# First attention of a gated two-layer network: preparation spread anew over its visits, value bias moved to the turned output

## The reference, cut to what matters

```python
kv = concat([y_main @ Wk + bk, y_main @ Wv + bv])      # per head 16 keys, 16 values
k = _ln(kv[..., :HD], kn_w, kn_b);  v = kv[..., HD:]
q = _ln((x @ Wq + bq).reshape(b, s1, H, HD), qn_w, qn_b)
ctx = _attn(q, k, v) + _attn(q, k_dca, v_dca)          # softmax(q k' * SCALE) v, each
x = x + tanh(g_xattn[0]) * (ctx @ Wo + bo)
```

## Time and profile before

| what | value |
|---|---|
| median of 3 runs | 1889.63 us (1887.51 to 1890.85) |
| profiled execution | 1893.01 us, its span 1891.3 us |
| mean granted TensorE clock | 0.981 of full speed |
| TensorE busy over the span | 1802.5 us (95%) |
| VectorE, ScalarE busy | 1420.0 us (75%), 1208.8 us (64%) |
| GpSimd busy | 352.2 us (19%) |

### The profile page before, as it was taken

How to read it: one execution, slowest core, us unless ns; L and a number is a source line. 1 busy time by engine, 2 the same in 40 slices (tenths; PEclk the granted TensorE clock), 3 DMA queues, 4 the chain that set the end, 5 groups by cost and what they waited for, 6 DMA issues and landing times.

```text
span 1891.3 us, 31855 instructions
## 1 busy us (share of the span) xinstructions
PE 1802.5 (95%) x9292; PEld 1334.9 (71%) x9292; DVE 1420.0 (75%) x2350; ACT 1208.8 (64%) x2035; POOL 352.2 (19%) x309
## 2 busy tenths in 40 slices
PE   5798898999999999999999999999999999999998
PEld 3444444568888767787777767778777777888887
DVE  8566656556666889897898988889889997666665
ACT  2576667853233778886888867888788885222222
POOL 3010101204444400001000010000100102454442
PEclk9799999989999999999999999999999999999999
DMA  3404141444443200001000010000000000544542
GB/s 98 109 19 109 32 96 35 93 159 126 111 116 89 70 1 1 0 0 35 1 1 0 0 35 1 1 0 0 1 22 1 0 17 16 114 109 106 116 114 75
DMA packets 108711, 95.90 MB, mean 51 GB/s; under 512 B 71796, under 2 KB 93176, under 8 KB 107992
## 3 DMA queue, kind: packets, MB, share of 16 engines
q1 hardware_dynamic: 108632, 94.88, 19.9%
HBM read 72.94 MB, written 1.44 MB: 39 GB/s over the span
## 4 chain that ended last, share of the span: by engine, by line
PE 83%; DVE 8%; ACT 2%; issue 2%; SPq 2%; POOL 1%; DMA 0%; DVEq 0%; ACTq 0%
PE ps L1308 36%; PE ps L472 17%; PE ps L484 8%; PE ps L1153 5%; PE ps L1140 4%; PE ps L1324 3%; PE ps L1078 2%; SPq L575 2%; PE ps L1389 1%; PE ps L1332 1%; PE ps L1417 1%; DVE s_rk L2015 1%; POOL s_p L811 1%; ACT s_p L1022 1%; DVE s_dsum L2091 1%
## 5 line engine op out<-in xcount | busy, mean ns | idle before, releaser
L1022 ACT ACTIVATE s_p<-ps,s_g,s_rk 128x256 f32<-128x256 f32 (+1 forms) x832 | 413.2, 561 | 8.9 <-DVE s_dsum L2091 7.6
L1308 PE MATMUL ps<-s_qq,s_ctxT 128*128 (+3 forms) x1248 | 357.9, 400 | 6.6 <-ACT s_p L1022 5.9
L472 PE MATMUL ps<-s_xT,s_wgus 128*128 128x512 f32 x1440 | 350.3, 392 | 0.0
L1308 PE MATMUL ps<-s_ps,s_ctx 128*128 128x512 f32 x1152 | 325.2, 395 | 0.9 <-DVE s_ps L2082 0.9
L472 PEld LDWEIGHTS ps<-s_xT,s_wgus 128*128 128x128 f32 x1440 | 271.2, 189 | 59.9 <-issue 1.5
L2082 DVE TENSOR_TENSOR s_ps<-s_p,s_ps 128x512 fp32r<-128x512 f32 x384 | 269.1, 701 | 20.8 <-ACT s_ps L1030 17.4
L899 ACT ACTIVATE s_p<-ps,s_bsm 128x1024 f32<-128x1024 f32 x208 | 219.5, 1111 | 88.7 <-PE ps L1153 86.3
L1308 PEld LDWEIGHTS ps<-s_qq,s_ctxT 128*128 128x128 f32 (+1 forms) x1248 | 224.0, 185 | 67.7 <-ACT s_p L1022 9.5
L1308 PEld LDWEIGHTS ps<-s_ps,s_ctx 128*128 128x128 f32 x1152 | 216.1, 188 | 56.6 <-DVE s_ps L2082 4.2
L2091 DVE TENSOR_TENSOR s_dsum<-s_dsum,s_p 128x512 f32<-128x512 f32 (+1 forms) x352 | 241.9, 687 | 16.5 <-ACT s_p L1022 12.8
L1886 DVE TENSOR_TENSOR s_hs<-s_hw,s_hs 128x512 fp32r<-128x512 f32 x120 | 140.6, 1172 | 80.6 <-ACT s_hs L383 80.6
(11 more groups left out here) (269 smaller groups left out, 2053.7 us busy)
## 6 DMA issues: line engine op xcount, KB each, us to landing
s_wB<-w1s SPq DMA_DIRECT2D x64, 256.0 KB, 3.9
s_kT<-s_kst SPq DMA_DIRECT2D x96, 128.0 KB, 2.4
s_kT<-s_kst SPq DMA_DIRECT2D x96, 80.0 KB, 2.1
s_wB<-w0s SPq DMA_DIRECT2D x15, 384.0 KB, 3.5
s_wB<-w0s SPq DMA_DIRECT2D x16, 256.0 KB, 3.8
s_wgu<-in_L_ffn_Wg_dram SPq DMA_DIRECT2D x64, 64.0 KB, 2.8
s_wgu<-in_L_ffn_Wu_dram SPq DMA_DIRECT2D x64, 64.0 KB, 2.5
s_wd<-in_L_ffn_Wd_dram SPq DMA_DIRECT2D x64, 64.0 KB, 2.4
```

Source lines behind the costliest of these rows:

```text
L472: ins = nc.tensor.matmul(ps[:, 4 + g, :], WGUS[f][:, slot, w, g, k, :], XT[f][:, x_, k, n], start=c == 0, stop=c == len(ops) - 1)
L1022: ins = nc.scalar.activation(p1[0:r, SLOT1[t], j, :], ps[0:r, BANK1[t], j * SQ:(j + 1) * SQ], ACT.Exp, bias=g1[0:r, 3:4], scale=rk_col(t, ...
L1308: ins = nc.tensor.matmul(out, lhs(x_), rhs(y_), start=first and n == 0, stop=last and n == 2)
```

## The change

1. `visit_work`: the 13 projections go two to a visit from visit 4 to 11 (where the second place isn't taken by `sums` or `query`); the keys of the next batch's half 0 go to visits 16 to 19, its query to visit 21. VectorE's list is reordered to match. `SQUARE` and `ROOT` move to earlier steps.
2. In a visit TensorE issues the values of the visit's first step before the second piece, not after it.
3. The bias of the values is not added to them. It is loaded as a column (`vb0`, 32 small loads), the two parts are summed, and it is added where the turned output is taken from PSUM.
4. In the prologue ScalarE copies the values of batch 0 and all four turned chunks of x; VectorE reads a tile only after ScalarE has (`v0_read`). ScalarE also writes the rounded part of the first keys; VectorE reads the first queries before the last two key tiles.
5. `center` multiplies and subtracts in one operation.

```diff
-TURN_ACT = (0, 2, 5, 7, 9)
-TURN_DVE = (0, 2, 3, 5, 7)
+TURN_ACT = (0, 4, 7, 9, 11)
+TURN_DVE = (0, 0, 1, 3, 5)
...
     if more:
-        first.update({4 + t: ("proj", b + 1, t) for t in range(KT)})
-        first.update({20: ("keys", b + 1, 0, 0), 21: ("query", b + 1, 0), 22: ("keys", b + 1, 0, 3)})
-        second.update({20: ("keys", b + 1, 0, 1), 21: ("keys", b + 1, 0, 2)})
+        places = [(work, u) for u in range(4, 12) for work in (first, second) if u not in work]
+        for t, (work, u) in enumerate(places[:KT]):
+            work[u] = ("proj", b + 1, t)
+        first.update({16 + c: ("keys", b + 1, 0, c) for c in range(4)})
+        first[21] = ("query", b + 1, 0)
...
-SQUARE = (18, 27, 35, 37)
-ROOT = 40
+SQUARE = (15, 21, 25, 28)
+ROOT = 32
...
+        def value_pieces(b, t):
+
+            pv = ps[:, misc_bank(MISC["proj", b, t]), :].rearrange("p (h two d) -> p h two d", two=2, d=D0)
+            return [(vg[r0:r0 + r, b % 2, tile, 0:H0 * (D0 + 1)].rearrange("p (h d) -> p h d", d=D0 + 1)[:, :, 0:D0], pv[r0:r0 + r, :, 1, :])
+                    for r0, r, tile in ([(0, P, t)] if t < KT - 1 else [(0, KREST, t), (DROW, DCA, KT)])]
...
+                if b == 0:
+                    for row in range(2):
+                        for c in range(KD):
+                            part = a["bkv0"][0, row, :].rearrange("(h two d) -> h two d", two=2, d=D0)[8 * c:8 * c + 8, 1, :]
+                            for h in range(8):
+                                sp.dma_start(vb0[D0 * h:D0 * h + D0, row, c:c + 1], part[h, :].rearrange("(p o) -> p o", o=1)).then_inc(s.vb_loaded, 16)
...
-            act_turn(act, 0)
+            def first_values(tiles):
+
+                for t in tiles:
+                    act.wait_ge(s.misc_made, MISC["proj", 0, t] + 1)
+                    for to, src in value_pieces(0, t):
+                        ins = nc.scalar.copy(to, src)
...
+                    ins.then_inc(s.v0_read, 1)
+
+            act_std(act, 0)
+            act.wait_ge(s.vg_ones, 1)
+            first_values(range(0, 4))
+            for half in range(2):
+                act_take(act, 0, half, (0, 1))
...
             for c in range(4):
+                if c < 3:
+                    first_values(range(4 * c + 4, min(4 * c + 8, KT)))
                 square(0, c)
...
-                    ins = nc.scalar.activation(p0[:, c, cols], ps[:, misc_bank(m), cols], ACT.Identity,
-                                               bias=wcol[:, 3 + 2 * j:4 + 2 * j], scale=wcol[:, 2 + 2 * j:3 + 2 * j])
+                    for to in (p0[:, c, cols], kst[:, 0, c * HALF + cols.start:c * HALF + cols.stop]):
+                        ins = nc.scalar.activation(to, ps[:, misc_bank(m), cols], ACT.Identity,
+                                                   bias=wcol[:, 3 + 2 * j:4 + 2 * j], scale=wcol[:, 2 + 2 * j:3 + 2 * j])
...
-                    prepare(second)
                     if tiles == 3:
                         scores_at(n + 5)
-                    for k in range(tiles):
+                    values(b, step)
+                    prepare(second)
+                    for k in range(1, tiles):
                         values(b, step + k)
...
+                if b == 0:
+                    dve.wait_ge(s.v0_read, t + 1)
...
-                me.did(v.tensor_tensor(kx[:, t], pv[:, :, 0, :], bv[:, :, 0, :], ALU.add))
-                if t < KT - 1:
-                    value(0, P, t).then_inc(s.misc_read, 1)
...
+                ins = v.tensor_tensor(kx[:, t], pv[:, :, 0, :], bv[:, :, 0, :], ALU.add)
+                if b:
+                    me.did(ins)
+                    pieces = value_pieces(b, t)
+                    for to, src in pieces:
+                        ins = v.tensor_copy(to, src)
...
-                cols = slice(starts[js[0]], starts[js[-1] + 1])
-                me.do(v.tensor_scalar(s1[:, cols], s1[:, cols], 1.0 / D0, None, ALU.mult))
                 for j in js:
-                    ins = v.tensor_tensor(centered[j][0], centered[j][0], bc(s1[:, starts[j]:starts[j + 1]], D0), ALU.subtract)
+                    ins = v.scalar_tensor_tensor(out=centered[j][0], in0=bc(s1[:, starts[j]:starts[j + 1]], D0), scalar=-1.0 / D0,
+                                                 in1=centered[j][0], op0=ALU.mult, op1=ALU.add)
...
-                v.tensor_copy(xnT[:, c, 0:HALF], ps[:, MISCBANK, :]).then_inc(s.misc_read, 1)
+                v.tensor_scalar(xnT[:, c, 0:HALF], ps[:, MISCBANK, :], vb0[:, 0, c:c + 1], None, ALU.add).then_inc(s.misc_read, 1)
```

More of the change, by code:

```diff
@@ L907, in _ @@
                 act.wait_ge(s.cx_turned, 4 * (c + 1))
-                nc.scalar.copy(xnT[:, c, HALF:2 * HALF], ps[:, 4 + c, :]).then_inc(s.cxT_act, 1)
+                if c == 0:
+                    act.wait_ge(s.misc_read, primed(MISC["ctx", 0] + 1))
+                nc.scalar.activation(xnT[:, c, HALF:2 * HALF], ps[:, 4 + c, :], ACT.Identity, bias=vb0[:, 0, c:c + 1]).then_inc(s.cxT_act, 1)
             def shares_exp(half):
@@ L1065, in bank_free @@
             def bank_free(m):
-                pe.wait_ge(s.misc_read, primed(m - 3 if m <= MISC["query", 0, 0] else m))
+                if m == MISC["query", 0, 0]:
+                    pe.wait_ge(s.kf_made, 1)
+                elif m < MISC["query", 0, 0]:
+                    pe.wait_ge(s.misc_read, primed(m - 3))
+                else:
+                    pe.wait_ge(s.misc_read, primed(m))
             def project(b, t):
@@ L1699, in read_keys @@
                 if b + half:
-                    dve.wait_ge(s.qz_ready, NG * b + (1 + (c == 3) if half else (c >= 2)))
+                    dve.wait_ge(s.qz_ready, NG * b + (1 + (c == 3) if half else 0))
                     dve.wait_ge(s.misc_made, m + 1)
@@ L1790, in _ @@
             scale_keys(0, 1)
-            for c in range(4):
-                read_keys(0, 0, c)
+            bounds()
+            read_keys(0, 0, 0)
+            read_keys(0, 0, 1)
+            dve.wait_ge(s.kf_made, 4)
+            dve.sem_inc(s.misc_read, 4)
             read_queries(0, 0)
-            bounds()
+            read_keys(0, 0, 2)
+            read_keys(0, 0, 3)
             for b in range(B):
@@ L1803, in _, with project @@
                 read_keys(b, 1, 3)
[L1804 to L1826 removed]
+                def project(tiles):
+                    if more:
+                        for t in tiles:
+                            read_projected(b + 1, t)
+                project(range(0, 4))
+                keep_sums(b, 0)
+                project(range(4, 7))
+                read_sums(b, 0)
+                if more:
+                    sum_squares(b + 1, 0)
+                project((7,))
+                read_queries(b, 2)
+                project((8, 9))
+                if more:
+                    sum_squares(b + 1, 1)
+                else:
+                    add_bias()
+                project(range(10, KT))
+                keep_sums(b, 1)
                 if more:
                     sum_squares(b + 1, 2)
+                read_sums(b, 1)
+                if more:
                     sum_squares(b + 1, 3)
                     key_variance(b + 1)
[L1831 removed]
+                read_queries(b, 3)
                 if more:
@@ L1835, in _ @@
                     scale_keys(b + 1, 1)
+                    read_keys(b + 1, 0, 0)
+                    read_keys(b + 1, 0, 1)
+                else:
+                    take_ctx(0)
+                    take_ctx(1)
+                keep_sums(b, 2)
+                if more:
+                    read_keys(b + 1, 0, 2)
+                    read_keys(b + 1, 0, 3)
                 read_sums(b, 2)
                 if more:
-                    read_keys(b + 1, 0, 0)
-                    read_keys(b + 1, 0, 1)
                     read_queries(b + 1, 0)
-                    read_keys(b + 1, 0, 2)
-                    read_keys(b + 1, 0, 3)
                 keep_sums(b, 3)
```

63 lines of the change are left out of this document (21 added, 42 removed).

## The result

The changed kernel takes **1885.55 us** (median of 11 runs, 1884.3 to 1887.65); the kernel before, on the same chips, 1891.73 (11 runs, 1887.21 to 1894.84). The ratio is 0.9969 with a 95% interval of 0.9959 to 0.9979: some 6 us, 0.31% faster. The forecast of 1876 asked for more than twice that; the time lies at the upper end of its whole range (1863 to 1886), above the 1871 to 1882 of the forecast proper, and within rival 4's 1885 to 1887.

A forecast was written before the change was run, and what follows sets the result against it. TensorE, busy 95% of the span, was taken as the bound, with gaps to close in the first attention. Terms -4.7 - 4.2 - 3.0 - 1.5 = -13.4 us took the median 1889.6 to 1876; range 1863 to 1886, forecast proper 1871 to 1882 (0.52).

The forecast's parts named there:

- rival 4: Change doesn't do what it says: batches stay at 90 us, prologue alone counts, 1885 to 1887; 0.20 together with rival 2.
- The prologue: Before the batches: VectorE's work passes to ScalarE, the reciprocal and first transfers come earlier; -4.7 us.
- Two projections in a visit: Visits 4 to 11: a values step covers VectorE's freeing of the bank, closing 0.48 gaps; -1.4 a batch, -4.2 in three.
- Start of a batch: Earlier keys end the transfer wait and values cover visit 0; gaps 2.3 become 1.25, -1.0 a batch, -3.0 in three.
- End of a batch: Visits 20 to 22 lose 3.2 us of gaps, VectorE's chain to the keys adds 2.7; -0.5 a batch, -1.5 in three.
- E: End of exponential 32 in a batch; next keys forecast ready at E+10.4, TensorE there at E+5.4 without any wait.
- Priced at nothing: 32 value-bias column loads (22 us of SyncE's queue), same-size replaced operations, the moved tanh and the bound's constants (1.2 us).
- Rival 1: The gaps go and no new one comes, query read over before E: -25.4 us, some 1864 to 1869; chance 0.20.
- Rival 2: Pairs stall: bank not free for the second projection, 0.48 five times a batch, 1883 or 1885; 0.20 together with rival 4.
- Rival 3: Chain behind the root: keys of visit 16 over 9.5 us late spend all other gains; 1897 at 12 us; chance 0.08.

The follow-up runs named there:

- e9: e8 with the prologue's constants of the exponent's bound moved behind the first query read, out of GpSimd's product; 1873.96 us, ratio 0.9915.
- e5: The kernel before with the split alone: a visit's first value step issued ahead of the second preparation piece; 1892.35 us, ratio 1.0011.
- e1: The changed kernel with a visit's values in one piece again, behind the second preparation piece; 1886.06 us, ratio 0.9972.
- e2: The changed kernel with values split only in visits that have two preparation pieces; 1880.63 us, ratio 0.9944.
- e11: e8 without any split, the values of every visit in one piece behind the second preparation piece; 1878.79 us, ratio 0.9931.
- e6: e2 with the next batch's four key pieces one visit later, in visits 17 to 20; 1872.90 us, ratio 0.9905.
- e7: e2 with the batch's last query turned in visit 12 instead of 14; 1874.44 us, ratio 0.9921.
- e8: e2 with both edits, keys in visits 17 to 20 and the last query in visit 12; 1872.86 us, ratio 0.9916.

## Why the prediction was right and wrong

**The prologue** (-4.7, bounds -3.0 to -5.5): right; -4.0 measured. VectorE's first read, tile 7, the query projections and the reciprocal came at 17.2, 22.4, 28.2 and 35.9 against 17.6, 22.65, 28.0 and 35.7. Mis-sized by 0.7 us were the constants of the bound, priced as free cover though a product of GpSimd's ran beside them; e9, with them moved, has its first exponential 1.0 us before that of after.

**Two projections in a visit** (-4.2): this is the step that failed, in its sentence "The matmuls are the same". They are the same in number; the split that the step counts as cover ("one step of values, 0.50 us, stands between too") was priced at nothing. Values in one piece of 16 hold TensorE 1.00 us, in two of 8 with a turn between them 1.14, and their neighbours lengthen too: 0.27 us in the visit shown above, and the edit splits 12 visits of batches 1 and 2, and 7 of the last, forecast at 64. That is +1.6 us in the last batch (shown by its rise in after and e5, and its return in e1 and e2), and 2.1 us more of TensorE's own time in batch 1. Of the gaps in visits 7, 8, 13 and 14, 1.9 us in batch 1, 1.1 came back as the expected 0.49 and an unexpected 0.60: -0.8 where -1.4 was forecast.

Added up from the terms (pairs, start and end of a batch), 1.9, 2.9, 2.9 and 1.0 us were forecast for the four batches, all of it idle time, and -1.8, -1.2, -0.75 and +1.6 came. Between equal points the account is this, in us, after less before:

| batch | idle | own time | sum |
|---|---|---|---|
| 0 | -3.2 | +1.4 | -1.8 |
| 1 | -3.3 | +2.1 | -1.2 |
| 2 | -2.9 | +2.15 | -0.75 |
| 3 | +0.3 | +1.3 | +1.6 |

The idle time fell by 9.1 us where the forecast has 8.7; TensorE's own time rose by 6.9 where it has nothing. With the 0.7 of the prologue that is the shortfall of 7.2. In batches 1 and 2 the clock was the same before and after, and in the last it was at full level, so there the rise isn't clock. In batch 0 the mean clock was 0.92 and 0.93, and how its rise divides between split and clock stays open. The removals of the split (e1, e2, e11) differ in clock too in batches 1 and 2, except for batch 1 of e11 beside that of e9.

**Start of a batch** (-1.0 each): right. No idle before the query of visit 2, whose key tile is no longer waiting for a transfer, and 0.87 where 1.0 was forecast. In batch 1 these gaps went from 2.3 to 1.1 us.

**End of a batch** (-0.5 each): the chain was right to half a microsecond (E+10.0, 4.6 us of gap). The gaps of batch 1's end went from 6.1 us to these 4.6, -1.5 where -0.5 was forecast, which makes up for what the pairs missed. What the forecast didn't see is what this gap governs. In the traces of after and e2 what is saved ahead of it in batches 1 and 2 is given back at it, as a wait or as slower matmuls: e2 saved splits and waits there, and the batches of its trace are no shorter. Taken away by a visit's delay (e6) or by an earlier query (e7), the kernel of e2 is 6 to 8 us faster. The bound "-3.2 if the query read lands well before E" describes what e7 builds: there only the 2.54 us of the table loads are left.

**Priced at nothing:** the 32 column loads cost 15.86 us of SyncE's queue (0.50 each, not 0.68), over at 95.5, 7 us before the next load is issued; hidden, as forecast.

**The rivals.** Rival 1 (1864 to 1869) needed the query out of the chain; with that built (e7, e8) the kernel gets to within 4 us of it. Rival 2's five stalls of 0.48 showed as a single one of 0.60 (the 0.49 stands behind a query's read and was in the forecast): wrong. Rival 3's chain stayed at 4.6 us, half of the point from which it decides. Rival 4 has the right time for the wrong reason: the batches didn't stay as they were, their gains and losses cancelled.

Both e6_late_keys and e8_both beat the kernels before and after: 1872.9 us, 17.5 below before and some 12 below after.

## What to carry to other kernels

Moving matmuls of one shape between matmuls of another isn't free on TensorE: before splitting a run, read the pace of starts of a whole and of a half run in the trace, and split only where a wait is sure to be covered. When a chain across engines sets the end of a stage, first find the wait it ends in and give it slack (ask later, or start it earlier); until then savings ahead of it may turn into a wait or into slower matmuls at it. And compare TensorE's busy time and granted clock of the same stretch before and after: equal work with more busy time is a cost that no list of waits shows.

## What the runs showed of the hardware

- Eight value matmuls (128*32 weights, 256 columns) hold TensorE 0.57 us and sixteen 1.00, and a run cut in two by a turn costs the visit 0.27 us, with no wait in the records. With ten such cuts in a batch, most of them at projections, TensorE's busy time is 1.2 us more (e9 beside e11, both at a mean clock of 0.98).
- TensorE's granted clock fell to the lower level (1.2 GHz) behind the table loads at the end of a batch: for 3.4 us from 213.1 in after, 10.2 us from 204.9 in e2 and not at all in batch 1 of e6, with gaps of 1.20 + 3.42, 1.76 + 0.58 and 1.76 + 0.29 + 0.88 us there. What decides between these isn't settled by these runs; beside e6 its price in e2 is 4 us of busy time a batch.
- Tiny operations aren't tiny beside GpSimd: `TENSOR_SCALAR` on 128x2 took 1.53 us beside GpSimd's product of two SBUF tiles and 0.17 to 0.23 away from it, each slow one ending within 0.03 us of the end of a product (43.33 and 43.31, 44.90 and 44.87); the query's cast took 1.97 instead of 0.69.
- A table load took 1.28 us, and the next activation stood right behind it (201.62 and 202.92).
